# One column of every fourth chunk of a graph gather fetched by 128 single-row transfers on SP's queue

## The chip, the cores and the metric

The kernel runs on one core of a Trainium2 chip. The metric is the device time of one execution in microseconds (us), the median of three runs. Beside the runs stands one execution recorded by the hardware profiler; the rows below are from it.

## The reference

Two layers of a graph network on 12,500 nodes with 128 features and 200,000 edges, sorted by target node. Only the first matters here:

```
h = relu(layernorm(x))
msgs = h[src]                                   # 200,000 rows of 128 floats
neigh = segment_sum(msgs, dst, 12500)
x = x + relu(relu(((1 + eps) * h + neigh) @ W1 + b1) @ W2 + b2)
h = relu(layernorm(x))
x = x + attention(h, src, dst, edge_attr, ...)  # the second sweep
```

## The kernel before

There are two sweeps over the edges, one after the other; the diff touches the first (`gin_sweeps`). The edges lie in 98 chunks of 2,048 (`NCH`, `CHUNK`): 16 columns (`COLS`) of 128 edges, one edge to a partition. Of a chunk's messages GpSimd (POOL) fetches one column with one indirect DMA: 128 rows of 512 bytes, each at an address taken from a list of indices, into one of four buffers `hs0` to `hs3` (`gather_chunk`, L513). The table `h0` (in the trace `h_rows`) is written to DRAM in the first 105 us; the first four chunks are gathered from `x` itself and normed on chip.

Each engine runs its own instruction stream over the same steps (`over_stages`): eight steps written out, a hardware loop over four steps at a time, and the last steps written out. A step is named by the chunk f that POOL gathers in it. The others work on chunks further back, and two names look ahead: a2 is chunk f+2, a1 is f+1, p0 is f-1, r4 is f-4, a5 is f-5.

- POOL, in step f: waits for the index list of f and for the sums of chunk f-4, makes one tiny multiplication (`hold`, L507), and issues 16 gathers.
- SP, in step f: loads the index list of chunk a2 once the gathers of a2-4 have landed (L604), fetches the nodes' own rows for p0 (L628), and stores what chunks a5 and r4 produced: source rows (L634), key columns (L637), one row of key biases (L639), residual rows (L645). The address of most of these is a number that SP first loads from a table on chip into a register (`spot`, L431). SP does all this in program order.
- PE (TensorE), for a chunk: waits until its gathers have landed, clears the sums (L689), and makes 16 multiplications of a column of messages with a one-hot matrix (L695), then the layer's products for earlier chunks. VectorE (DVE) adds the sums to the accumulator (`add_sums`, L918); ScalarE (ACT) evicts and norms.

What SP does in a step, cut to its transfers:

```
if a2 and (a2.at is None or a2.at > 7): list_of(a2)
sp.dma_start(x[m.j][:, :, :], rows_at(a["x"], at))       # m = p0
sp.dma_start(rows_at(arow, at), A[m.j][:, :, :])         # m = a5
sp.dma_start(qk[:, bass.ds(at, MW)], kq[m.j][:, :])
sp.dma_start(ck[:, bass.ds(at, MW)], cq[m.j][:, :])
sp.dma_start(rows_at(res, at), r[m.j][:, :, :])          # m = r4
```

Of the kernel before, what the change touches and what calls it, by code (L numbers as in the profile page):

```python
# [67 lines left out]
MT = 2  # L68
MW = MT * P
STEPS = 7  # L70
assert (NCH - MID_PEEL) % 4 == 2 and 2 ** STEPS >= NCH and NCH * P == NP and NP >= MW
assert TILES % (2 * GT) == 0 and NBLK % PB == 0 and NCH % 4 == 2 and HALF <= 512

# [162 lines left out]
def head(nc, a, g, first, qk, ck, raw0, raw1, idx, weights):  # L236
# [4 lines left out]
    with ExitStack() as ctx:  # L241
# [29 lines left out]
        @block.sync  # L271
        def _(sp):
            sp.dma_start(g["idx0"][:, :], a["src_chunks"][0:1].rearrange("a p k -> p (a k)")).then_inc(idx_in, 16)
            sp.dma_start(by_block[:, :, :], a["dst_blocks"].rearrange("(k p) e -> p k e", p=PB)).then_inc(blocks_in, 16)
            sp.dma_start(idx[1][:, :], a["src_chunks"][1]).then_inc(idx1_in, 16)
            sp.dma_start(by_edge[:, :, :], a["dst_cols"].rearrange("p (b s) -> p b s", s=SUB)).then_inc(dst_in, 16)
            sp.dma_start(g["eps1"][:, :], a["eps"].to_broadcast([P, 1])).then_inc(eps_in, 16)
            for tile, rows in weights:
                sp.dma_start(tile[:, :], rows).then_inc(g["weights_in"], 16)
            for n in range(2, 5):  # L280
                sp.dma_start(idx[n % 4][:, :], a["src_chunks"][n]).then_inc(lists_in, 16)
            sp.wait_ge(zero_ready, 1)
            sp.dma_start(qk[:, NP:NW], zero[:, :]).then_inc(g["keys_out"], 16)
            sp.dma_start(ck[:, NP:NW], zero[0:1, :]).then_inc(g["keys_out"], 16)
            sp.wait_ge(start_ready, 2)
            sp.dma_start(first, start[:, :]).then_inc(g["start_out"], 16)
            sp.wait_ge(g["keys_out"], 32)
            sp.wait_ge(lists_in, 48)

        @block.gpsimd  # L290
        def _(gp):
# [222 lines left out]
                              in_offset=bass.IndirectOffsetOnAxis(ap=idx[:, k:k + 1], axis=0)).then_inc(done, 16)  # L514


def gin_sweeps(nc, a, g, h0, first, res, arow, qk, ck):


# [2 lines left out]
    with ExitStack() as ctx:  # L522
# [6 lines left out]
        weights += [(W[k], a[k]) for k in ("W1", "W2", "Wq", "WkT")]  # L529
        weights += [(W[k], a[k].rearrange("(a d) -> a d", a=1).to_broadcast([P, D])) for k in ("b2", "bt")]  # L530
        weights += [(col[k], a[k].rearrange("(d a) -> d a", a=1)) for k in ("b1", "bq", "bk", "gamma", "beta")]
        head(nc, a, g, first, qk, ck, raw0, raw1, idx, weights)
        span = nc.values_load(g["span"][0:1, 0:1], min_val=0, max_val=N + WIN)
        hs = [st.sb(f"hs{k}", [P, COLS, D]) for k in range(4)]
# [8 lines left out]
        kq, cq = st.two("kq", [P, MW]), st.two("cq", [1, MW])  # L543
        m1, m2 = moment_buffers(st, g, "m1"), moment_buffers(st, g, "m2")
        zeros = st.sb("zeros", [1, SPAN], BF16)
        sums = [st.ps(f"sums{j}") for j in range(2)]
        uy_bank, ta_bank, qk_bank, c_bank = (st.ps(k) for k in ("uy_bank", "ta_bank", "qk_bank", "c_bank"))
        u_ps, y_ps = uy_bank[:, 0:MW], uy_bank[:, MW:2 * MW]
# [4 lines left out]
        capped = hs[3][0:1, :, :].rearrange("p k d -> p (k d)")[:, 0:NBLK + NCH]  # L553
        w = {"capped": st.sem("w_capped"), "tables": st.sem("w_tables"), "spread": st.sem("w_spread")}
        held, lists_again = st.sem("held"), st.sem("lists_again")
        idx_in, gathered = ([st.sem(f"{k}_{n}") for n in range(4)] for k in ("idx_in", "gathered"))
        x_in, r_out, a_out, q_out = st.sem2("x_in"), st.sem2("r_out"), st.sem2("a_out"), st.sem2("q_out")
        hot_ready, sums_ready, added = st.sem("hot_ready"), st.sem("sums_ready"), st.sem("added")
# [10 lines left out]
        pe_regs = [nc.tensor.alloc_register(f"gin_win{b}") for b in range(BPC)]  # L569
        x_reg, r_reg, a_reg = (nc.sync.alloc_register(f"gin_{k}") for k in ("x_spot", "r_spot", "a_spot"))  # L570
        u_reg = nc.tensor.alloc_register("gin_u_spot")

        nc.vector.tensor_copy(g["spot"][:, :], g["spots"][0][:, :]).then_inc(spot_ready, 1)
        nc.vector.wait_ge(spot_ready, 1)
# [6 lines left out]
        x_groups = a["x"].rearrange("(g t p) d -> g p t d", t=GT, p=P)  # L581
        h_groups = h0.rearrange("(g t p) d -> g p t d", t=GT, p=P)
        one = lambda rows, G: rows[G:G + 1].rearrange("a p t d -> p (a t) d")
        landed = lambda m: 16 * (COLS * (m.g + (1 if m.k else 0)) - (AHEAD if m.k == 1 else 0))
        tail = [st.sem(f"tail{q}") for q in range(QUADS - 1)]
        listed = lambda m: 16 * (m.g - (0 if m.k else 1))
        raw_row = lambda n, k: raw0[:, k, :] if n == 0 else raw1[:, k, :] if n == 1 and k < AHEAD else hs[n % 4][:, k, :]
# [3 lines left out]
        with nc.Fori(0, span + 1, WIN):  # L591
            with nc.Block() as block:
                @block.sync
                def _(sp):
# [11 lines left out]
                    def first_lists():  # L606
                        for m in range(NCH - 4, NCH - 1):
                            sp.wait_ge(gathered[m % 4], landed(Chunk(None, m)))
                        for q in range(QUADS - 1):
                            sp.wait_ge(tail[q], 64)  # L610
                        for n in range(1, 5):
                            sp.dma_start(idx[n % 4][:, :], src[n]).then_inc(lists_again, 16)

                    def step(a2, a1, f, p0, p1, p2, r4, a5):
                        if a2 and a2.at is not None and 3 < a2.at < 7:
                            list_of(Chunk(None, a2.at + 1))
                        if a2 and (a2.at is None or a2.at > 7):
                            list_of(a2)
                        if f and f.at == 0:
                            for G in range(GROUPS):  # L620
                                node_rows(G)
                        if p0:
                            m = p0
                            if m.at == 0:
                                sp.wait_ge(w["tables"], 7)
                            at = spot(sp, x_reg, g, m.c)
                            wait(sp, s["x1"], m.c - 1)
                            sp.dma_start(x[m.j][:, :, :], rows_at(a["x"], at)).then_inc(x_in[m.j], 16)  # L628
                        if a5:
                            m = a5  # L630
                            at = spot(sp, a_reg, g, m.c)
                            wait_alone(sp, w["tables"], a_out[1 - m.j], 16 * (m.h + m.j))
                            wait(sp, s["a_sb"], m.c + 1)
                            sp.dma_start(rows_at(arow, at), A[m.j][:, :, :]).then_inc(a_out[m.j], 16)  # L634
                            wait_alone(sp, w["tables"], q_out[1 - m.j], 32 * (m.h + m.j))
                            wait(sp, s["k_sb"], m.c + 1)
                            sp.dma_start(qk[:, bass.ds(at, MW)], kq[m.j][:, :]).then_inc(keys_out if m.last else q_out[m.j], 16)  # L637
                            wait(sp, s["c_sb"], m.c + 1)
                            sp.dma_start(ck[:, bass.ds(at, MW)], cq[m.j][:, :]).then_inc(keys_out if m.last else q_out[m.j], 16)  # L639
                        if r4:  # L640
                            m = r4
                            at = spot(sp, r_reg, g, m.c)
                            wait_alone(sp, w["tables"], r_out[1 - m.j], 16 * (m.h + m.j))
                            wait(sp, s["r"], m.c + 1)
                            sp.dma_start(rows_at(res, at), r[m.j][:, :, :]).then_inc(r_out[m.j], 16)  # L645
                        if p2 and p2.at == NCH - 1:
                            first_lists()
                    over_stages(sp, step, 6, MID_PEEL, 2)
# [7 lines left out]
                def _(gp):  # L656
                    def step(f, bk, p1, p2, r4, a5):
                        if f and f.at != 0:
                            if f.at == 3:
                                gp.wait_ge(w["tables"], 7)  # L660
                            if f.at == RAW:
                                for u in range(4):
                                    gp.wait_ge(h_out[u], 16 * len(range(u, GROUPS, 4)))
                            wait(gp, idx_in[f.k], listed(f))
                            wait(gp, sums_ready, f.c - 3)
                            hold(gp, g, held, f.c - 1)
                            if f.last:
                                for q in range(QUADS - 1):
                                    gather_chunk(gp, idx[f.k], h0, hs[f.k], tail[q], cols=range(4 * q, 4 * q + 4))
                            else:  # L670
                                gather_chunk(gp, idx[f.k], a["x"] if f.at is not None and f.at < RAW else h0, hs[f.k], gathered[f.k],
                                             cols=range(AHEAD if f.at == 1 else 0, COLS))
                    over_stages(gp, step, 6, MID_PEEL)

                @block.tensor
                def _(pe):
# [3 lines left out]
                    def add_rows(bk):  # L680
# [9 lines left out]
                        for b in range(BPC):  # L690
# [1 line left out]
                            if bk.last and b % 2 == 0 and b // 2 < QUADS - 1:  # L692
                                pe.wait_ge(tail[b // 2], 64)
                            for k in range(b * SUB, (b + 1) * SUB):
                                mm = pe.matmul(sums[j][:, bass.ds(off, WIN)], hs[bk.k][:, k, :], hot[j][:, k, :],  # L695
                                               start=False, stop=True, skip_group_check=True)
                        mm.then_inc(sums_ready, 1)

# [65 lines left out]
                def _(act):  # L764
# [68 lines left out]
                            act.activation(hn[:, t, :], h2[:, t, :], ACT.Identity, bias=m2["shift"][:, t:t + 1],  # L833
                                           scale=m2["rstd"][:, t:t + 1]).then_inc(s["hn"], 1)

                    def step(f, bk, p1, p2, r4, a5):
                        if f and f.at == 0:
                            edge_rows(0)
                            for G in range(GROUPS):
# [23 lines left out]
                            norm2(p1)  # L863
                        if f and f.at is not None and 0 < f.at < RAW:
                            edge_rows(f.at)
                    over_stages(act, step, 6, MID_PEEL)

                @block.vector
                def _(v):
# [650 lines left out]
```

## Time and profile before

| what | us |
|---|---|
| median of 3 runs (lowest to highest) | 4064.28 (4064.09 to 4066.64) |
| the profiled execution | 4065.53 |
| its span, first to last instruction | 4063.9 |
| POOL busy, whole span | 3025.3 |
| PE busy, whole span | 3316.0 |

The span is 1.6 us shorter than the execution's time. A row of a timeline gives start and duration in us and the engine; SPq is SP issuing a transfer (the transfer itself goes on after that), POOL's gathers likewise. What stands in brackets is how long the engine was idle before, and what ended that; "issue" means that it waited for nothing that the profile shows. A row of a line's or tile's answer gives the smallest, median and largest duration in ns of its instructions; MOVE, FUSED_REGOPS and TENSOR_LOAD are the queue's own register instructions, the last a read of numbers from a table on chip into registers.

### The profile page before, as it was taken

To read this page: it belongs to the slowest core of one execution; us is meant where nothing else is said; L and a number is where in the kernel's file an instruction comes from. 1 tells how busy PE (TensorE), PEld (TensorE's weight loads), DVE (VectorE), ACT (ScalarE), POOL (GpSimd) and SP (SyncE) were. 2 spreads that over 40 slices of the span, in tenths; PEclk is the share of its full clock that TensorE was granted. 3 is DMA by queue.
4 is the path that set the end of the run, shared out by engine and by line. 5 is a ranking of instruction groups with operands and counts; after the bars stand their busy time and mean duration, and the time that the engine had idled before them with its cause. 6 is when DMAs were issued, how large, how long until landed. Compare 5 with 4: busy or idle time off the path is not lost.

```text
span 4063.9 us, 75137 instructions
## 1 busy us (share of the span) xinstructions
PE 3316.0 (82%) x19120; PEld 2587.6 (64%) x19121; DVE 1932.2 (48%) x6898; ACT 1590.9 (39%) x3223; POOL 3025.3 (74%) x3332
## 2 busy tenths in 40 slices
PE   1697777777767777777779999999999999999998
PEld 1465555555555555555557777777777777777776
DVE  5433222222222222222256666666666666666666
ACT  6433222222222222222244444444444444444444
POOL 6677777777777777777577777777777777777773
PEclk6555555555555555555589999999999999999998
DMA  6233333233333233333244444544454444444443
GB/s 189 70 83 82 80 79 79 78 79 78 79 78 78 79 79 78 79 78 79 72 124 140 139 140 137 142 136 142 134 141 140 140 139 138 139 139 139 139 139 91
DMA packets 390065, 446.29 MB, mean 110 GB/s; under 512 B 111768, under 2 KB 314734, under 8 KB 390000
## 3 DMA queue, kind: packets, MB, share of 16 engines
q0 software_dynamic: 100096, 205.20, 20.1%
q1 hardware_dynamic: 276940, 233.83, 19.4%
q10 hardware_dynamic: 12964, 6.53, 0.5%
q8 instruction: 25, 0.41, 0.0%
q14 instruction: 40, 0.33, 0.0%
HBM read 387.05 MB, written 58.21 MB: 110 GB/s over the span
## 4 chain that ended last, share of the span: by engine, by line
POOL 26%; issue 10%; PE 8%; DMA 4%; DVE 1%; SPq 1%; DVEq 0%; POOLq 0%; ACT 0%; ACTq 0%
POOL attention_t L513 26%; DMA attention_t<-source_rows,attention_idx 2%; PE attention_sc_q L1164 2%; PE attention_pre_ps L1141 2%; DMA attention_idx<-in_src_chunks 1%; PE attention_t_ps L1150 1%; PE attention_pre_ps L1137 1%; PE attention_sum_ps L1207 1%; PE attention_row_bank L1186 0%; PE attention_xm_bank L1227 0%; PE attention_xm_bank L1226 0%; DVE attention_masked L1431 0%; POOL spare L507 0%; SPq L1097 0%; DVE attention_rr L1454 0%
## 5 line engine op out<-in xcount | busy, mean ns | idle before, releaser
L513 POOL DMA_INDIRECT attention_t<-source_rows,attention_idx x1548 | 1478.4, 955 | 457.0 <-issue 448.1
L513 POOL DMA_INDIRECT gin_hs<-h_rows,gin_idx x1500 | 1428.6, 952 | 443.7 <-issue 443.4
L695 PE MATMUL gin_sums<-gin_hot,gin_hs 128*128 128x40 f32 x3136 | 684.8, 412 | 0.0
L695 PEld LDWEIGHTS gin_sums<-gin_hot,gin_hs 128*128 128x128 f32 x3136 | 670.4, 329 | 22.4 <-issue 21.9
L1278 ACT ACTIVATE attention_tT<-attention_pre_ps 128x512 f32<-128x512 f32 x391 | 233.5, 597 | 881.4 <-PE attention_pre_ps L1141 881.3
L1141 PE MATMUL attention_pre_ps<-attention_evT,attention_w_edge 128*128 128x512 f32 x782 | 419.7, 619 | 1.7 <-issue 1.7
L1164 PE MATMUL attention_sc_q<-attention_qw,attention_tT 128*128 x3128 | 410.9, 275 | 0.0
L1164 PEld LDWEIGHTS attention_sc_q<-attention_qw,attention_tT 128*128 128x128 f32 x3128 | 389.4, 196 | 0.0
L918 DVE TENSOR_TENSOR acc<-acc,gin_sums 128x264 f32 x98 | 42.1, 430 | 684.7 <-PE gin_sums L695 682.6
L1207 PE MATMUL attention_sum_ps<-attention_e_hot,attention_t 128*128 128x96 f32 x3072 | 365.9, 277 | 0.0
L1207 PEld LDWEIGHTS attention_sum_ps<-attention_e_hot,attention_t 128*128 128x128 f32 x3072 | 350.2, 192 | 11.9
L1137 PE MATMUL attention_pre_ps<-ident,attention_t 128*128 128x128 f32 x1564 | 255.9, 288 | 119.6 <-DMA attention_t<-source_rows,attention_idx 114.5
L798 ACT ACTIVATE gin_n_zT<-gin_c_bank,eps 128x256 f32<-128x256 f32 x98 | 46.5, 474 | 672.4 <-PE gin_c_bank L713 672.4
L1150 PEld LDWEIGHTS attention_t_ps<-ident,attention_tT 128*128 128x128 f32 x1564 | 195.2, 145 | 176.6 <-issue 167.1
L1416 DVE TENSOR_TENSOR attention_lines<-attention_lines,attention_row_bank 1x40 f32 x784 | 144.3, 184 | 337.3 <-issue 146.8
L689 PE MATMUL gin_sums<-gin_zeros 1*128 1x264 bf16 x98 | 36.4, 371 | 325.9 <-DMA gin_hs<-h_rows,gin_idx 293.7
L1137 PEld LDWEIGHTS attention_pre_ps<-ident,attention_t 128*128 128x128 f32 x1564 | 175.7, 145 | 161.3 <-issue 118.3
L689 PEld LDWEIGHTS gin_sums<-gin_zeros 1*128 1x128 bf16 x98 | 9.7, 99 | 399.0 <-issue 399.0
L1431 DVE TENSOR_TENSOR attention_masked<-attention_masked,attention_row_bank 128x80 f32<-128x80 f32 x784 | 126.6, 231 | 267.6 <-PE attention_row_bank L1186 267.3
L1150 PE MATMUL attention_t_ps<-ident,attention_tT 128*128 128x128 f32 x1564 | 245.9, 281 | 0.0
L1282 ACT ACTIVATE attention_t<-attention_t_ps 128x512 f32<-128x512 f32 x391 | 231.8, 593 | 27.2 <-PE attention_t_ps L1150 27.1
L491 ACT ACTIVATE gin_m_std<-gin_m_mv,ln_eps 128x2 f32<-128x2 f32 x294 | 85.1, 290 | 343.0 <-DVE gin_m_mv L485 342.5
(215 smaller groups left out, 5151.0 us busy)
## 6 DMA issues: line engine op xcount, KB each, us to landing
attention_evT<-in_edge_attr_cols SPq DMA_DIRECT2D x196, 512.0 KB
attention_t<-source_rows,attention_idx POOLq DMA_INDIRECT x1548
gin_hs<-h_rows,gin_idx POOLq DMA_INDIRECT x1500, 2.5
attention_qw<-qk_cols SPq DMA_DIRECT2D x98, 160.0 KB
attention_cw<-qk_bias_cols SPq DMA_DIRECT2D x98, 132.0 KB
attention_fade<-fades SPq DMA_DIRECT2D x98, 132.0 KB
gin_x<-in_x SPq DMA_DIRECT2D x98, 128.0 KB, 2.2
residual_rows<-gin_r SPq DMA_DIRECT2D x98, 128.0 KB, 2.1
```

Of the source, the lines that this page charges most:

```text
L491: act.activation(m["std"][:, :], m["mv"][:, :, 1], ACT.Sqrt, bias=g["ln_eps"][:, 0:1]).then_inc(s["std"], 1)
L513: gp.indirect_dma_start(out=out[:, k, :], out_offset=None, in_=rows[:, :], compute_op=op, in_offset=bass.IndirectOffsetOnAxis(ap=idx[:, k: ...
L695: mm = pe.matmul(sums[j][:, bass.ds(off, WIN)], hs[bk.k][:, k, :], hot[j][:, k, :], start=False, stop=True, skip_group_check=True)
L1137: pe.matmul(pre_ps[:, k * P:(k + 1) * P], t[f.k][:, 4 * q + k, :], g["ident"][:, :], is_transpose=True, start=(k == 0), stop=False, skip_g ...
L1141: pe.matmul(pre_ps[:, :], w_edge[:, :], evT[q // 2][:, 512 * (q % 2):512 * (q % 2 + 1)], start=False, stop=True, skip_group_check=True).th ...
L1150: mm = pe.transpose(t_ps[:, k * P:(k + 1) * P], tT[q % 2][:, k * P:(k + 1) * P], g["ident"][:, :])
L1164: mm = pe.matmul(sc_ps[:, o:o + WIDE], tT[q % 2][:, (n % 4) * P:(n % 4 + 1) * P], qw[j][:, bass.ds(off, WIDE)], start=True, stop=True)
L1207: mm = pe.matmul(sum_of(bk)[:, bass.ds(off, WIDE)], t[bk.k][:, k, :], e_hot[j][:, k, :], start=False, stop=True, skip_group_check=True)
L1278: act.activation(tT[q % 2][:, :], pre_ps[:, :], ACT.Gelu).then_inc(s["tT_sb"], 1)
L1282: act.activation(t[f.k][:, 4 * q:4 * q + 4, :].rearrange("p k d -> p (k d)"), t_ps[:, :], ACT.Copy).then_inc(s["t_sb"], 1)
L1416: v.tensor_tensor(some, some, row_bank[0:1, b * WIN:(b + 1) * WIN], ALU.max).then_inc(s["raised"], 1)
L1431: v.tensor_tensor(masked[j][:, cols, :], masked[j][:, cols, :], row_bank[:, bass.ds(off, WIN)].unsqueeze(1).to_broadcast([P, SUB, WIN]), A ...
```

## The change

For each fourth chunk from chunk 7 on (7, 11, ... 95: 23 chunks), column 15 is no longer gathered by POOL. SP loads that column's row numbers from a new list on chip (`lone_list`, 3,072 numbers, loaded once at the start), eight at a time into eight registers, and issues one transfer of one row (512 bytes, one partition) for each, 128 in all, into a new buffer `lone`. The 128 are split over four steps of SP: 32 at the end of the steps in which the chunk is a2, a1, f and p0. The first of the four waits for the sums of the chunk four before, which still reads `lone`. PE waits for the four quarters ahead of the chunk's last multiplication and reads `lone` in place of `hs`. `BY_ACT` is empty, so ACT issues none; its extra code does nothing. The cut diff:

```diff
+LONE = 3
+BY_SP, BY_ACT = (32, 32, 32, 32), ()
...
+            sp.dma_start(g["lone_list"][:, :], a["src_lone"]).then_inc(lists_in, 16)
...
+def alone(m):
+    return m is not None and m.k == LONE and (m.at is None or m.at > LONE)
+
+def rows_alone(eng, regs, g, m, table, out, spots, done):
+    for at in range(0, len(spots), len(regs)):
+        some = spots[at:at + len(regs)]
+        eng.load(regs[:len(some)], g["lone_list"][0:1, bass.ds(m.g * P + some[0], len(some))])
+        for reg, p in zip(regs, some):
+            row = eng.snap(reg, min_val=0, max_val=NP - 1)
+            eng.dma_start(out[p:p + 1, :], table[bass.ds(row, 1), :]).then_inc(done, 16)
...
+        g["lone_list"] = st.sb("lone_list", [1, NCH // 4 * P], I32)
+        lone = st.sb("lone", [P, D])
+        sp_rows, act_rows = ([e.alloc_register(f"gin_{k}_row{b}") for b in range(8)] for e, k in ((nc.sync, "sp"), (nc.scalar, "act")))
...
+                    def lone_rows(m, u):
+                        if u == 0:
+                            wait(sp, sums_ready, m.c - 3)
+                        if u == 0 and m.at == LONE + 4:
+                            for k in range(4):
+                                sp.wait_ge(h_out[k], 16 * len(range(k, GROUPS, 4)))
+                        at = sum(BY_SP[:u])
+                        rows_alone(sp, sp_rows, g, m, h0, lone, range(at, at + BY_SP[u]), lone_sp[u])
...
                             sp.dma_start(rows_at(res, at), r[m.j][:, :, :]).then_inc(r_out[m.j], 16)
+                        for u, m in enumerate((a2, a1, f, p0)):
+                            if alone(m):
+                                lone_rows(m, u)
...
-                                             cols=range(AHEAD if f.at == 1 else 0, COLS))
+                                             cols=range(AHEAD if f.at == 1 else 0, COLS - 1 if alone(f) else COLS))
...
-                                mm = pe.matmul(sums[j][:, bass.ds(off, WIN)], hs[bk.k][:, k, :], hot[j][:, k, :],
+                                by_row = alone(bk) and k == COLS - 1
+                                if by_row:
+                                    for u, n in enumerate(BY_SP):
+                                        wait(pe, lone_sp[u], 16 * n * bk.g)
...
+                                mm = pe.matmul(sums[j][:, bass.ds(off, WIN)], lone[:, :] if by_row else hs[bk.k][:, k, :], hot[j][:, k, :],
```

The line numbers below are each kernel's own; L513 of before is L517 in the change.

SP, one step of the loop. In the kernel before it is this, from the index list to the row of key biases, behind which the residual store (L645) ends the step:

```order
L604 DMA gin_idx<-in_src_chunks 128x16
L431 ISA
L431 TENSOR_LOAD pos
L628 ISA
L628 DMA gin_x<-in_x 128x2x128
L431 TENSOR_LOAD pos
L634 ISA
L634 DMA source_rows<-gin_A 128x2x128
L637 REGISTER_ALU
L637 DMA qk_cols<-gin_kq 128x256
L639 DMA qk_bias_cols<-gin_cq 1x256
```

In the change, from the residual store (L678, before L645) on, the same step goes on with one load of eight numbers and eight times an ISA (register arithmetic) and a one-row transfer, and that four times over, ahead of the next step's list:

```order
L678 DMA residual_rows<-gin_r 128x2x128
L530 ISA
L530 TENSOR_LOAD gin_lone_list
L532 ISA
L533 DMA gin_lone<-h_rows 1x128
L532 ISA
L533 DMA gin_lone<-h_rows 1x128
```

So each step of SP from 5 to 96 has 32 transfers, 32 register instructions and 4 loads more than before.

POOL, one turn of the loop in the change (four chunks). Before, each of the four rows of gathers reads x16:

```order
L517 DMA gin_hs<-h_rows,gin_idx 128x128 x16
L82 REGISTER_ALU
L511 TENSOR_TENSOR spare<-ones 1x1
L517 DMA gin_hs<-h_rows,gin_idx 128x128 x16
L82 REGISTER_ALU
L511 TENSOR_TENSOR spare<-ones 1x1
L517 DMA gin_hs<-h_rows,gin_idx 128x128 x15
L141 REGISTER_ALU
```

One gather of 64 is gone in each turn.

## Rows read from the trace of the kernel before

**Rows 1.** The page: slices of the span, PE, POOL and the granted clock.

```profile
PE   1697777777767777777779999999999999999998
...
POOL 6677777777777777777577777777777777777773
PEclk6555555555555555555589999999999999999998
```

**Rows 2.** Busy time of each engine in one stretch, in the first sweep.

```profile
core 0: us, PE busy (x) PEld busy (x) DVE busy (x) ACT busy (x) POOL busy (x), PEclk, DMA share, GB/s
400.00:1900.00 1500.00, 1089.41 (x4108) 836.92 (x4109) 424.68 (x1780) 416.05 (x1117) 1146.83 (x1267) 0.55 0.31 79
```

**Rows 3.** Timeline of POOL in the first sweep, from one chunk's end to the next.

```profile
1003.14 0.22 POOL L507 TENSOR_TENSOR spare<-ones 1x1 f32<-1x1 f32 x1
1003.52 0.98 POOL L513 DMA_INDIRECT gin_hs<-h_rows,gin_idx  x1 [0.15 <-issue]
1004.80 0.94 POOL L513 DMA_INDIRECT gin_hs<-h_rows,gin_idx  x1 [0.30 <-issue]
1006.05 0.95 POOL L513 DMA_INDIRECT gin_hs<-h_rows,gin_idx  x1 [0.30 <-issue]
...
1023.59 0.98 POOL L513 DMA_INDIRECT gin_hs<-h_rows,gin_idx  x1 [0.15 <-issue]
```

**Rows 4.** Who waited for whom, 340 to 1950 us: POOL, PE, SP's queue.

```profile
POOL gin_hs L513 <- issue: 377.8, 1280, 0.3
...
PE gin_sums L689 <- DMA gin_hs<-h_rows,gin_idx: 282.0, 72, 5.0
...
SPq L604 <- DMA gin_hs<-h_rows,gin_idx: 1191.6, 80, 16.1
```

**Rows 5.** Timeline of SP's queue, two steps of the first sweep.

```profile
1004.93 0.38 SPq L604 DMA_DIRECT2D gin_idx<-in_src_chunks  x1
1005.97 0.40 SPq L628 DMA_DIRECT2D gin_x<-in_x  x1
1006.99 0.40 SPq L634 DMA_DIRECT2D source_rows<-gin_A  x1
1007.63 0.37 SPq L637 DMA_DIRECT2D qk_cols<-gin_kq  x1
1008.09 0.29 SPq L639 DMA_DIRECT2D qk_bias_cols<-gin_cq  x1
1009.54 0.39 SPq L645 DMA_DIRECT2D residual_rows<-gin_r  x1
1024.96 0.37 SPq L604 DMA_DIRECT2D gin_idx<-in_src_chunks  x1
...
1029.37 0.38 SPq L645 DMA_DIRECT2D residual_rows<-gin_r  x1
```

**Rows 6.** Two one-row transfers on SP's queue, all instances: min/median/max ns.

```profile
L639 SPq DMA_DIRECT2D qk_bias_cols<-gin_cq x98: 283/292/324, 166.0 to 2035.9; - x98
...
L1037 SPq DMA_DIRECT2D attention_bv<-in_bv x1: 288/288/288, 2038.9 to 2038.9; - x1
```

**Rows 7.** Timeline of SP's queue in the second sweep, two transfers with register arithmetic between.

```profile
2528.69 0.33 SPq L1074 DMA_DIRECT2D attention_wgt<-in_wgt_cols  x1
2529.22 0.33 SPq L1080 DMA_DIRECT2D attention_qw<-qk_cols  x1
```

**Rows 8.** Loads of registers from a table: one number on SP, eight on PE.

```profile
L450 SPq TENSOR_LOAD <-places x98: 263/270/452, 2053.0 to 3987.3; - x98
...
L455 PEldq TENSOR_LOAD <-places x196: 587/592/1028, 48.3 to 4007.5; - x196
```

**Rows 9.** Timeline of DVE: adding the sums of chunks 3, 7, 8, 95 and 97.

```profile
174.93 0.43 DVE L918 TENSOR_TENSOR acc<-acc,gin_sums 128x264 f32 x1 [4.30 <-PE gin_sums L695]
...
237.62 0.43 DVE L918 TENSOR_TENSOR acc<-acc,gin_sums 128x264 f32 x1 [4.10 <-PE gin_sums L695]
254.25 0.43 DVE L918 TENSOR_TENSOR acc<-acc,gin_sums 128x264 f32 x1 [4.08 <-PE gin_sums L695]
...
1979.34 0.43 DVE L918 TENSOR_TENSOR acc<-acc,gin_sums 128x264 f32 x1 [7.36 <-PE gin_sums L695]
...
2016.63 0.43 DVE L918 TENSOR_TENSOR acc<-acc,gin_sums 128x264 f32 x1 [4.11 <-PE gin_sums L695]
```

**Rows 10.** The index lists (L604) on SP's queue: from issue to landing.

```profile
DMA to landing us min/median/max: 1.6/1.7/6.0
```

More of the change, by code:

```diff
@@ L70 @@
 STEPS = 7
+LONE = 3
+BY_SP, BY_ACT = (32, 32, 32, 32), ()
+assert sum(BY_SP) + sum(BY_ACT) == P
 assert (NCH - MID_PEEL) % 4 == 2 and 2 ** STEPS >= NCH and NCH * P == NP and NP >= MW
@@ L287, in _ @@
             sp.wait_ge(g["keys_out"], 32)
-            sp.wait_ge(lists_in, 48)
+            sp.wait_ge(lists_in, 64)
         @block.gpsimd
@@ L555, in gin_sweeps @@
         held, lists_again = st.sem("held"), st.sem("lists_again")
+        lone_sp, lone_act = ([st.sem(f"{k}_{u}") for u in range(len(n))] for k, n in (("lone_sp", BY_SP), ("lone_act", BY_ACT)))
         idx_in, gathered = ([st.sem(f"{k}_{n}") for n in range(4)] for k in ("idx_in", "gathered"))
@@ L583, in gin_sweeps @@
         one = lambda rows, G: rows[G:G + 1].rearrange("a p t d -> p (a t) d")
-        landed = lambda m: 16 * (COLS * (m.g + (1 if m.k else 0)) - (AHEAD if m.k == 1 else 0))
+        landed = lambda m: (16 * ((COLS - 1) * m.g + COLS) if m.k == LONE else
+                            16 * (COLS * (m.g + (1 if m.k else 0)) - (AHEAD if m.k == 1 else 0)))
         tail = [st.sem(f"tail{q}") for q in range(QUADS - 1)]
@@ L694, in add_rows @@
                             for k in range(b * SUB, (b + 1) * SUB):
-                                mm = pe.matmul(sums[j][:, bass.ds(off, WIN)], hs[bk.k][:, k, :], hot[j][:, k, :],
+                                by_row = alone(bk) and k == COLS - 1
+                                if by_row:
+                                    for u, n in enumerate(BY_SP):
+                                        wait(pe, lone_sp[u], 16 * n * bk.g)
+                                    for u, n in enumerate(BY_ACT):
+                                        wait(pe, lone_act[u], 16 * n * bk.g)
+                                mm = pe.matmul(sums[j][:, bass.ds(off, WIN)], lone[:, :] if by_row else hs[bk.k][:, k, :], hot[j][:, k, :],
                                                start=False, stop=True, skip_group_check=True)
@@ L834, in norm2, with lone_rows, step @@
                                            scale=m2["rstd"][:, t:t + 1]).then_inc(s["hn"], 1)
-                    def step(f, bk, p1, p2, r4, a5):
+                    def lone_rows(m, u):
+                        if u == 0:
+                            wait(act, sums_ready, m.c - 3)
+                        if u == 0 and m.at == LONE + 4:
+                            for k in range(4):
+                                act.wait_ge(h_out[k], 16 * len(range(k, GROUPS, 4)))
+                        at = sum(BY_SP) + sum(BY_ACT[:u])
+                        rows_alone(act, act_rows, g, m, h0, lone, range(at, at + BY_ACT[u]), lone_act[u])
+                    def step(a2, a1, f, bk, p1, p2, r4, a5):
                         if f and f.at == 0:
@@ L865, in step @@
                             edge_rows(f.at)
-                    over_stages(act, step, 6, MID_PEEL)
+                        for u, m in zip(range(len(BY_ACT)), (a2, a1, f)):
+                            if alone(m):
+                                lone_rows(m, u)
+                    over_stages(act, step, 6, MID_PEEL, 2)
                 @block.vector
@@ L1501 @@
         "src_chunks": np.ascontiguousarray(chunked(src, 0).reshape(NCH, P, COLS)),
+        "src_lone": np.ascontiguousarray(chunked(src, 0).reshape(NCH, P, COLS)[LONE::4, :, COLS - 1]).reshape(1, NCH // 4 * P),
         "dst_cols": cols(chunked(dst, N)),
```

## The prediction

> **What bounds the kernel now.** I read the slices first: PE is busy at seven tenths and more through the first half and nine in the second, POOL at seven throughout [rows 1]. The change touches the first half alone, so the averages of the page say nothing about it, and I took a stretch of the first sweep by itself: there POOL is busy 1147 of 1500 us and PE 1089, at a granted clock of 0.55 [rows 2], close to the lower of TensorE's two levels (1.2 of 2.4 GHz). Neither is full, so the waits must decide. POOL waits for nothing but "issue", 0.3 us before each gather [rows 3, 4]: its gathers follow each other every 1.25 us (1004.80, 1006.05), 16 of them with the tiny multiplication in about 20.05 us (1003.52 to 1023.59). PE waits for POOL's gathers, 282 us in 72 waits, and SP for the same, 1191.6 us in 80 [rows 4]. So a step of the first sweep is POOL's 20 us, PE has about 4 us of slack in it, and SP about 15.
>
> **What goes.** 23 gathers at 1.25 us [rows 3] are 28.7 us off POOL's stream. While POOL is the bound, this is the whole gain: 0.7%.
>
> **What SP gets.** Its stream is what I price, since SP does everything in order and each of its 92 steps from 5 to 96 gets 32 rows and 4 loads.
>
> - Its own work in a step runs from the list to the end of the residual store: 5.00 us in one step (1004.93 to 1009.93) and 4.79 in the next [rows 5], 4.9 on average, with 0.19 of register instructions ahead of the first transfer: **5.1 us**. It waits in it for the gathers alone.
> - A row: the transfer itself holds SP's queue 0.29 us, as both one-row transfers of the trace do, with a constant address and with one from a register [rows 6]. Between two transfers of which the second has a new address worked out in registers, the gap is 2529.22 - 2529.02 = 0.19 to 0.20 us [rows 7]. The change has exactly this between its rows (one ISA each), so 0.29 + 0.19 = **0.48 us a row**, 15.4 us for 32. The lowest row is the step from L637 to L639, which use one address: 0.09 us between, 0.38 a row [rows 5]. That is not this pattern, and I keep it for a rival.
> - A load of eight numbers: none on SP in the trace. On PE eight take 0.59 us, on SP one takes 0.27 [rows 8], so eight cost about 0.32 more. From L628 to L634 the gap is 0.62 with a one-number load in it, without the 0.19 of register work 0.43: the lower end, as if eight cost what one does. Behind the one-row store L639 the gap is 1.16 [rows 5]; less 0.19 and plus 0.32 that is 1.29, the upper end. The middle, 0.43 + 0.32 = 0.75, has no delay behind a one-row transfer; three of four loads stand behind one, but the 1.16 also holds more waits than the 0.62. I take **0.95 us**, 3.8 for four.
>
> The step of SP is then 5.1 + 15.4 + 3.8 = **24.3 us**, and POOL's would be about 19.7 (20.05 less a quarter of 1.25). SP becomes the bound, and the 28.7 us on POOL are worth nothing: POOL will wait for sums or lists.
>
> **Who waits.** PE needs the last quarter of a chunk's rows ahead of its last multiplication; SP issues it at the end of the step before. With SP late, PE stands in front of that multiplication in each fourth chunk, and the other three run at PE's own pace, which has room: 16.63 us from chunk 7 to 8, when POOL was ahead [rows 9]. SP's new wait, for the sums of the chunk before that used `lone`, should cost little: they come 1.7 us of landing [rows 10] plus under 1 us after the last row, and SP meanwhile does 5.1 us of its own step. If that cover failed, at most 5 us in each of 23 chunks would be added. PE's four extra waits and the list's load at the start (one transfer more, ahead of a wait of SP for other engines' tables) I cost at nothing: PE waits there anyway, and the start's price, uncovered, is one transfer, some 0.4 us [rows 5].
>
> **The sum.** The first rows can go when chunk 3 is summed, 174.93 us, in step 5 [rows 9]: its batch takes 19.2 us, to 194.6. Then 91 steps of 24.3 us: 2211.3, so the last row is issued at 2405.9. With 1.7 us to land and 0.9 for multiplication and adding, the sums of chunk 95 are added at 2408.5, where they were at 1979.3. The last two chunks are gathered by then and go at PE's 16.63 us each, 2441.8 for chunk 97, where it was 2016.63 [rows 9]. So the second sweep starts 425 us later. It isn't touched. Against the profiled execution's 4065.5 us, which is 1.3 above the median of the runs, that is **4490 us**, 10% slower.
>
> **Bounds.** With loads at 0.43 the step is 22.2 us, 92 times 2.1 less: 4297. With 1.29 it is 25.7: 4615. A row off by 0.01 us is 0.32 a step and 29 us in all. That gives 4270 to 4645.
>
> **Rival 1: hidden, faster.** If SP's batch stays under 19.7 - 5.1 = 14.6 us (0.46 us a row, its share of a load included), POOL stays the bound and the time is 4065.5 - 28.7 = 4037. For it: SP idles 15 us in a step now [rows 4], and with the lowest rows, 0.38 a row and 0.43 / 8 = 0.05 for its load, a batch is 13.8 us. Against it: each row has its own address, and the four loads at their lower end with rows of 0.48 already make 17.1 us. The Trainium skill, "DMA: Bandwidth & Descriptors", section "Issuing engines are not separate DMA queues", has the rule behind this rival: the sequencer's time to start a transfer is "usually small relative to the DMA itself"; by it the time is 4037. The trace speaks against leaning on it: a list needs 1.7 us to land, but SP has issued the next transfer by then [rows 5, 10], so of many small transfers in a row the issue is what adds up. Chance 0.06.
>
> **Rival 2: each row holds up the next, much slower.** The gap behind the one-row store is 1.16 us where the gap with the same kind of load behind a larger transfer is 0.62 [rows 5]. If some 0.4 us of that were a stall after every one-row transfer, which decides as soon as it hits rows and not loads alone, a row is 0.88, a step 37.1 us, and 92 times 12.8 more makes 5668. Against it: a transfer only sends, and what was seen to be late is a load, which must read. The Trainium skill, same page, section "Why a DMA increments its semaphore by 16 and not by 1", says that of a transfer spread over fewer than 16 engines the issuing sequencer writes the rest of the increment itself; no row here shows how many engines a one-row transfer uses. Chance 0.08.
>
> **Rival 3: even.** Costs that meet near 14.6 us a batch: within 0.2% of 4065, about 8 us, which is what a measurement of this kernel can tell from no change. The window is narrow, 14.6 us give or take 0.1. Chance 0.02. That the change does not do what it says is no rival: the order shows 15 gathers and 128 one-row transfers in each turn of the loop.
>
> **Chances.** The forecast has 0.84, rival 1 0.06, rival 2 0.08, rival 3 0.02. Faster 0.06, same 0.02, slower 0.92. The range is the forecast's own, 4270 to 4645; it leaves out the rivals, 0.16, and a little of the forecast's edges.
>
> **What would show it.** In the profile after: steps of SP's queue in the first sweep 24 us apart from list to list, with no idle time before the list (the 1191.6 us of waits on gathers gone); one-row transfers 0.48 us apart within eight, about 1.4 from one eight to the next; PE waiting for transfers into `lone` in each fourth chunk; POOL waiting for sums or lists where it waited for nothing; 23 gathers fewer; the second sweep as long as before. Rows under 0.4 us apart and SP still waiting for gathers would mean rival 1; rows 0.9 apart rival 2. Loads much off 0.95 move the time by 92 x 4 = 368 times the difference.

## The result, and the profile after

| | before | after |
|---|---|---|
| median, us (runs) | 4064.42 (4) | 4354.85 (4) |
| lowest to highest, us | 4064.09 to 4066.64 | 4351.46 to 4356.85 |
| ratio, 95% interval | | 1.0718 [1.0706, 1.0731] |
| profiled execution and its span, us | 4065.53, 4063.9 | 4354.31, 4352.7 |

The change makes the kernel 290 us slower. The forecast was 4490 us in a range of 4270 to 4645: the direction and the mechanism came as foretold, the size was 135 us too large.

The page after, slices of the span and the engines' sums:

```profile
PE 3237.3 (74%) x19120; PEld 2506.3 (58%) x19121; DVE 1931.4 (44%) x6898; ACT 1590.9 (37%) x3223; POOL 3020.6 (69%) x3309
...
PE   1765556654755556566557999999999999999998
...
POOL 6666666666666666666634777777777777777774
...
PEclk5555655556565555655566999999999999999998
```

PE stood at seven tenths and more in the first sweep and POOL at seven [rows 1]; now PE mostly shows five and six and POOL six. No engine that counts as "busy" has become fuller. Only the queue that issues has, and that one has no line on the page. A second change is easy to miss: a slice is 109 us now and was 102, and yet the first sweep ends in the 22nd slice, where it ended in the 20th; from there on the slices look as before.

The waits show it. Who waited for whom after, 340 to 2200 us (engine, line, releaser: us in total, times, longest):

```profile
PE gin_sums L737 <- DMA gin_lone<-h_rows: 433.9, 21, 24.6
DVE gin_A L957 <- DMA source_rows<-gin_A: 429.9, 60, 10.1
...
POOL gin_hs L517 <- issue: 405.7, 1283, 0.5
...
POOL spare L511 <- DMA gin_idx<-in_src_chunks: 187.2, 76, 3.2
...
POOL spare L511 <- PE gin_sums L737: 13.4, 5, 2.9
```

PE's 282 us of waits for gathers [rows 4] are gone from the list, and so are SP's 1191.6: the same question for SP's queue has no row at all. In their place PE stands in front of the last multiplication of each fourth chunk, 434 / 21 = 20.7 us each time, and POOL, which waited for nothing, waits 187 us for index lists that SP issues late. DVE's 430 us belong to SP as well: its stores of source rows are late, so their buffers come free late. That last one I had not foreseen. The time follows SP's step alone in the runs below, so I take it to cost nothing of its own; no run tests it by itself.

SP's queue itself, timeline after, two steps of the loop (start, duration, x32 is 32 transfers from the first one's start to the last one's end):

```profile
1013.20 0.37 SPq L628 DMA_DIRECT2D gin_idx<-in_src_chunks  x1
1014.42 0.40 SPq L661 DMA_DIRECT2D gin_x<-in_x  x1
...
1017.79 0.38 SPq L678 DMA_DIRECT2D residual_rows<-gin_r  x1
1019.23 16.30 SPq L533 DMA_DIRECT2D gin_lone<-h_rows  x32
1035.84 0.37 SPq L628 DMA_DIRECT2D gin_idx<-in_src_chunks  x1
...
1041.77 16.31 SPq L533 DMA_DIRECT2D gin_lone<-h_rows  x32
1059.04 0.38 SPq L628 DMA_DIRECT2D gin_idx<-in_src_chunks  x1
```

SP works through without a pause. Its own part, list to the end of the residual store, is 1018.17 - 1013.20 = 4.97 us (5.00 and 4.79 before, [rows 5]). From there to the end of the last row, the batch, it is 1035.53 - 1018.17 = **17.36 us**, and 0.31 more to the next list. In the second step that gap is 0.96 (1058.08 to 1059.04). Over the steps between 340 and 1880 us the three parts are 5.05, 17.35 and 0.45 us on average, 22.85 together. The gap is 0.97 in every fourth step and 0.2 to 0.3 in the others; the loop has four steps to a turn, but whether its turn is the cause no run shows.

How long one row takes is seen in narrower pieces of the same timeline (the first eight rows, the eighth alone, and the ninth, behind the next load), and in all instances of the three lines (smallest, median and largest duration in ns):

```profile
1019.23 3.29 SPq L533 DMA_DIRECT2D gin_lone<-h_rows  x8
1022.29 0.23 SPq L533 DMA_DIRECT2D gin_lone<-h_rows  x1
1023.54 0.27 SPq L533 DMA_DIRECT2D gin_lone<-h_rows  x1
```

```profile
L533 SPq DMA_DIRECT2D gin_lone<-h_rows x2944: 224/228/324, 174.8 to 2270.2; - x197
...
L530 SPq TENSOR_LOAD <-gin_lone_list x368: 533/694/852, 174.1 to 2263.7; - x184
...
L532 SPq FUSED_REGOPS  x2944: 44/44/56, 174.7 to 2270.1; - x197
```

A row holds the queue 0.228 us (the first of a load's eight up to 0.32). From the first row of the eight to the eighth it is 22.29 - 19.23 = 3.06; less 0.08 for the longer first one that is 0.426 us a row. From the eighth to the ninth it is 1.25, with a load of 0.69 in it: a load costs 1.25 - 0.43 + 0.08 = 0.90 us more than a row alone. All in all the 92 batches run from 174.8 to 2270.2: less 16.1 for the last batch's own rows, (2095.4 - 16.1) / 91 = **22.85 us a step**, where the gathers had set 19.92 (the lists from 198.0 to 1930.9 us, 87 steps; MOVE is the register instruction ahead of each list with a computed address). The lists before:

```profile
L604 SPq MOVE gin_idx<-in_src_chunks x88: 29/29/29, 198.0 to 1930.9; - x88
```

The sums of chunks 95 and 97, DVE after (in brackets the idle time before and what ended it):

```profile
2272.31 0.43 DVE L972 TENSOR_TENSOR acc<-acc,gin_sums 128x264 f32 x1 [15.86 <-PE gin_sums L737]
...
2305.44 0.43 DVE L972 TENSOR_TENSOR acc<-acc,gin_sums 128x264 f32 x1 [4.13 <-PE gin_sums L737]
```

Before, 97 was added at 2016.63 [rows 9]. From there to the end of the span it was 2047.3 us (4063.9 - 2016.63), and it is 2047.3 now (4352.7 - 2305.44). The whole 289 us lie in the first sweep; that they are SP's is what the experiments test.

### The profile page after: what moved, and what is told of

Its sections match the earlier page's. It is cut to its first block and busy times, and to the rows that moved or that the text cites. A ratio compares the mean times of both kernels' runs of the same rounds, so it can differ in the third digit from the quotient of the medians.

```text
span 4352.7 us, 84781 instructions
## 1 busy us (share of the span) xinstructions
PE 3237.3 (74%) x19120; PEld 2506.3 (58%) x19121; DVE 1931.4 (44%) x6898; ACT 1590.9 (37%) x3223; POOL 3020.6 (69%) x3309
## 3 DMA queue, kind: packets, MB, share of 16 engines
q14 instruction: 152, 1.25, 0.1%
## 5 line engine op out<-in xcount | busy, mean ns | idle before, releaser
L517 POOL DMA_INDIRECT attention_t<-source_rows,attention_idx x1548 | 1477.1, 954 | 456.9 <-issue 449.9
L517 POOL DMA_INDIRECT gin_hs<-h_rows,gin_idx x1477 | 1425.7, 965 | 465.9 <-issue 465.6
L737 PE MATMUL gin_sums<-gin_hot,gin_hs 128*128 128x40 f32 x3090 | 594.3, 379 | 0.0
L737 PEld LDWEIGHTS gin_sums<-gin_hot,gin_hs 128*128 128x128 f32 x3090 | 580.6, 293 | 19.1 <-issue 14.9
L737 PE MATMUL gin_sums<-gin_hot,gin_lone 128*128 128x40 f32 x46 | 14.3, 411 | 475.7 <-DMA gin_lone<-h_rows 475.7
L737 PEld LDWEIGHTS gin_sums<-gin_hot,gin_lone 128*128 128x128 f32 x46 | 11.5, 312 | 478.2 <-issue 478.2
L511 POOL TENSOR_TENSOR spare<-ones 1x1 f32<-1x1 f32 x195 | 36.9, 189 | 331.4 <-DMA gin_idx<-in_src_chunks 202.8
L957 DVE TENSOR_TENSOR gin_A<-gin_ta_bank,gin_w_bt 128x256 f32<-128x256 f32 x98 | 40.7, 415 | 495.2 <-DMA source_rows<-gin_A 491.6
```

Source lines behind the costliest of these rows:

```text
L517: gp.indirect_dma_start(out=out[:, k, :], out_offset=None, in_=rows[:, :], compute_op=op, in_offset=bass.IndirectOffsetOnAxis(ap=idx[:, k: ...
L737: mm = pe.matmul(sums[j][:, bass.ds(off, WIN)], lone[:, :] if by_row else hs[bk.k][:, k, :], hot[j][:, k, :], start=False, stop=True, skip ...
```

## The experiments

All are edits of the changed kernel. The theory: SP's stream of instructions sets the step. The main rival: something else that the change brought (PE's wait in front of the last multiplication, the chunk's own latency, the missing gathers' place) does. Ratios are to the kernel before in runs on the same chip: 4064.42 us beside the change, 4071.61 beside e1_pool16, e_rows112, e_rows96 and e_mix, 4078.24 beside the other four; they lie up to 0.001 from the quotients of the medians shown here. "Batch" is read from one step of each profile as above, from the end of the residual store to the end of the last row; "step" is the time from the first list with a computed address to the last, divided by 87. The profiled executions of e_rows96 (4059.57) and e_mix4 (4030.08) were the highest and the lowest of their runs, so their steps carry that spread.

| kernel | SP's rows a step, loads | batch, us | step, us | median, us | ratio [95%] |
|---|---|---|---|---|---|
| the change | 32, 4 | 17.36 | 22.9 | 4354.85 | 1.0718 [1.0706, 1.0731] |
| e1_pool16 | 32, 4 | 17.37 | 22.8 | 4354.77 | 1.0701 [1.0684, 1.0717] |
| e_load16 | 32, 2 | 16.61 | 22.2 | 4304.98 | 1.0555 [1.0535, 1.0574] |
| e_mix | 23, 3 | 15.73 (12.82 in each fourth, 15.0 on average) | 20.5 | 4139.78 | 1.0171 [1.0157, 1.0185] |
| e_rows112 | 28, 4 | 15.09 | 20.7 | 4154.2 | 1.0207 [1.0192, 1.0223] |
| e_scaled8 | 32, 4 | 14.94 | 20.3 | 4125.36 | 1.0125 [1.0107, 1.0142] |
| e_scaled16 | 32, 2 | 13.92 | 19.6 | 4052.97 | 0.9946 [0.9931, 0.9962] |
| e_rows96 | 24, 3 | 12.98 | 19.6 | 4044.09 | 0.9924 [0.991, 0.9937] |
| e_mix4 | 24 and 20, 3 | 12.93 | 19.3 | 4043.23 | 0.992 [0.9906, 0.9935] |

**e1_pool16: POOL gathers all 16 columns again, SP still fetches the rows.** PE still waits for `lone`, but multiplies the gathered column.

```diff
...
-  cols=range(AHEAD if f.at == 1 else 0, COLS - 1 if alone(f) else COLS)
+  cols=range(AHEAD if f.at == 1 else 0, COLS)
...
-  mm = pe.matmul(..., lone[:, :] if by_row else hs[bk.k][:, k, :], ...)
+  mm = pe.matmul(..., hs[bk.k][:, k, :], ...)
```

> SP issues and PE awaits the 128 one-row transfers as in the change, but POOL gathers all 16 columns again and PE multiplies the gathered column. Theory (SP's issue work sets the step, 22.9 us, POOL's 20.05 us fits below it): the 23 gathers that were saved are worth nothing, so 4355 us, give or take 10. Rival A (POOL's stream still sets part of the time beside SP): the 28.7 us come back on top, 4383. Rival B (contention of row transfers with gathers is the cost): more than 4383.

The 23 gathers taken from POOL are worth nothing while SP sets the step: the medians are 4354.77 and 4354.85 us and the two intervals overlap, though POOL has all its old work; 28.7 us more would have been 0.007 more in the ratio. POOL had time to spare: between 340 and 1900 us it waits 159 us for index lists in the change and still 113 us here.

```profile
POOL spare L511 <- DMA gin_idx<-in_src_chunks: 113.0, 60, 2.8
```

That is the prediction's "the 28.7 us on POOL are worth nothing", shown.

**e_rows112 and e_rows96: fewer rows.** SP fetches 112 and 96 of the 128 rows; the last 16 and 32 are left out of the sums (zeros in their place).

```diff
-BY_SP, BY_ACT = (32, 32, 32, 32), ()
+BY_SP, BY_ACT = (28, 28, 28, 28), ()      # e_rows96: (24, 24, 24, 24)
...
+        nc.vector.memset(lone[:, :], 0.0).then_inc(spot_ready, 1)
```

> 28 rows a step in place of 32; the last 16 rows of the column are left out (zeros are added for them). Theory: SP's step shrinks by 4 x 0.42 and a little of the last load, to about 21.0 us, still over POOL's 19.75; 92 x 1.85 less, about 4185 us. Rival (PE's wait for the landing of late one-row transfers is the cost, whatever their number): above 4300.

> 24 rows and 3 loads a step; the last 32 rows of the column are left out (zeros are added for them). Theory: SP's step shrinks by 8 x 0.42 and one load group of 0.86 to about 18.6 us, under POOL's 19.75, so POOL is the bound again and the saved gathers count: 4064 - 29 = 4036 us. Rival (waiting for the landing): still slower than 4064.

From 32 rows to 28 the step falls by 2.2 us and the time by some 200, 92 times that; I had expected 1.85 and 170, so four rows are worth more than the price of a row and of the shorter load accounts for, and why is open. From 28 to 24 the batch loses 2.1 us more, the step only 1.1: it has reached POOL's. With 24 rows SP waits again. SP's queue in e_rows96, 340 to 1900 us:

```profile
SPq L628 <- DMA gin_hs<-h_rows,gin_idx: 59.6, 44, 2.8
SPq L529 <- PE gin_sums L737: 45.9, 15, 3.1
```

And then the change's gain is there: 0.9924 with an interval of 0.991 to 0.9937, where 28.7 us of 4065 would be 0.9929. All other parts of the change (the buffer, PE's waits, SP's new wait) are still in this kernel, so none of them costs more than about 0.1% of the time, the room that the interval leaves.

**e_mix: all 128 rows, 36 of them issued by ACT.**

```diff
-BY_SP, BY_ACT = (32, 32, 32, 32), ()
+BY_SP, BY_ACT = (23, 23, 23, 23), (12, 12, 12)
```

> All 128 rows, 23 a step on SP in four steps and 12 a step on ACT in three. Theory: SP's step is about 18.2 us, hidden; ACT gets some 6.5 us at the end of its step, in which it idles about 7.5 us before the next sums: hidden or nearly, 4036 to 4050. Rival (ACT's lateness reaches PE's chain): each of 69 ACT batches costs up to 6.5 us beyond PE's 3.5 us of slack, some 4100 to 4250.

A miss, and 4139.78 us lies in the range that I had given to the rival, ACT. But SP has fewer rows than in e_rows96 and yet a longer batch. What got longer is its loads. All loads in e_mix, and beside them those of e_rows112:

```profile
L530 SPq TENSOR_LOAD <-gin_lone_list x276: 541/1799/2003, 173.8 to 2048.8; - x138
...
L530 ACTq TENSOR_LOAD <-gin_lone_list x138: 500/617/747, 186.3 to 2028.3; - x138
```

```profile
L529 SPq TENSOR_LOAD <-gin_lone_list x368: 461/692/875, 169.6 to 2063.6; - x184
```

A load on SP takes 1.80 us at the median here and 0.69 there. With batches of 23 the loads of the first step begin at places 0, 8 and 16 of the chunk's list, those of the other three at 23, 46 and 69 and onward by eight: none of these is a multiple of four. Within the one kernel, loads of 8, 8 and 7 numbers each time, first in a step of the second kind and then in the one of the first kind:

```profile
L530 SPq TENSOR_LOAD <-gin_lone_list x3: 1633/1839/1899, 1013.3 to 1024.3; - x3
...
L530 SPq TENSOR_LOAD <-gin_lone_list x3: 698/824/1099, 1077.3 to 1085.9; - x3
```

So the place from which a load reads seems to decide, at equal sizes. A multiple of eight is not needed: in e_rows112 batches begin at 28 and 84 too, and its loads take 0.69 at the median and 0.875 at most. The next run tests it; why it is so, no run shows.

**e_mix4: the same with every load at a multiple of four.**

```diff
+BY_SP, BY_ACT = (24, 24, 24, 20), (12, 12, 12)
```

> As the mixed run, but with 24, 24, 24 and 20 rows a step on SP and 12 on ACT in three, so that each load of eight numbers begins at a multiple of four numbers in the list. In the mixed run SP's loads took 1.8 us where they began at odd multiples and 0.7 elsewhere. Theory (the place of the numbers is what made them slow): loads at 0.7 us, SP's step about 18.6 us, under POOL's 19.75: 23 gathers less, about 0.992 of before. Rival (ACT's issuing beside SP made SP's loads slow, or ACT's batch delays PE): still 1.01 to 1.02 of before.

ACT issues the same 36 rows as in e_mix, so it was not ACT that cost the time there. SP's loads are back at 0.70 us, SP waits again, and this is the best version with all 128 rows:

```profile
L530 SPq TENSOR_LOAD <-gin_lone_list x276: 462/696/827, 173.6 to 1931.2; - x138
```

```profile
SPq L628 <- DMA gin_hs<-h_rows,gin_idx: 70.6, 45, 2.4
SPq L530 <- PE gin_sums L737: 50.1, 20, 3.1
```

It beats the kernel before by 0.8% and the change by 7%: the idea of the change is good for what POOL saves, as long as SP's part of the rows fits into POOL's step.

**e_load16: sixteen numbers a load.** Two loads a step in place of four.

```diff
-  sp_rows, act_rows = ([e.alloc_register(f"gin_{k}_row{b}") for b in range(8)] ...
+  sp_rows, act_rows = ([e.alloc_register(f"gin_{k}_row{b}") for b in range(16)] ...
```

> All 128 rows on SP, loaded by two loads of 16 numbers a step in place of four of eight. Theory (the step is the sum of SP's instructions): a load of 16 takes 0.69 + 8 x 0.04 = 1.0 us, so the step falls by 4 x 0.86 - 2 x 1.17 = 1.1 us to 21.8, 92 x 1.1 = 101 us less: about 1.047 of before. Rival (SP's loads are hidden behind its transfers, which set the pace): 1.07 as the change.

Faster than the change, by less than I expected: the step falls by 0.6 us and not by 1.1, mostly since a load of sixteen takes 1.19 us, not 1.0, twice a step. The rest is the gap ahead of the next list, 0.56 us here on average and 0.45 in the change; its cause is open. All loads of e_load16:

```profile
L530 SPq TENSOR_LOAD <-gin_lone_list x184: 987/1194/1312, 171.8 to 2201.8; - x184
```

**e_scaled8 and e_scaled16: less register work a row.** The list is multiplied once, on DVE at the start, by a row's 512 bytes, and the table is read as bytes. Then the register holds the place itself, and in the trace one register instruction of some 0.15 us serves eight rows, in place of one of 0.044 us for each; the same in e_scaled16, which also has e_load16's edit and so two behind each load.

```diff
...
+    flat = table.rearrange("(a n) d -> a (n d)", a=1).bitcast(U8)
...
+        places = [eng.snap(reg, min_val=0, max_val=(NP - 1) * ROW) for reg in regs[:len(some)]]
+        for place, p in zip(places, some):
+            eng.dma_start(out[p:p + 1, :].bitcast(U8), flat[:, bass.ds(place, ROW)]).then_inc(done, 16)
...
+        nc.vector.tensor_scalar(g["lone_list"][:, :], g["lone_list"][:, :], float(ROW), None, ALU.mult).then_inc(spot_ready, 1)
```

> All 128 rows on SP; the list is multiplied by the row's 512 bytes once, by DVE at the start, and the address is used as loaded, so one register instruction for eight rows takes the place of one for each row. Theory: a row falls from 0.42 to about 0.33 us, the step by some 2.5 us to 20.3 to 20.8, still over POOL's 19.75: 1.013 to 1.026 of before. Rival (the transfer itself sets the pace, the register work is hidden): 1.07 as the change.

> The scaled list and loads of 16 together. Theory: both savings add, step 19.2 to 19.7 us, just under POOL's: all 128 rows on SP are hidden and the 23 gathers count, 0.992 to 1.003 of before. Rival: the savings don't add, over 1.01.

Both came as expected, e_scaled8 at the lower edge. SP's queue in e_scaled16, sixteen rows behind one load, and the waits of POOL and PE, 340 to 1900 us:

```profile
1000.72 5.28 SPq L536 DMA_DIRECT2D gin_lone<-h_rows  x16
```

```profile
POOL gin_hs L519 <- issue: 362.2, 1226, 0.3
POOL gin_hs L519 <- DMA gin_idx<-in_src_chunks: 1.8, 6, 0.3
...
PE gin_sums L741 <- DMA gin_lone<-h_rows: 248.8, 20, 14.7
```

Less 0.23 for the last transfer and 0.08 for the longer first one, 4.97 us for 15 rows are 0.33 us a row; so the register instruction of 44 ns and the gap that it brings cost 0.43 - 0.33 = 0.10 us of every row (the transfer itself still holds the queue 0.228 us at the median). The 0.15 us ahead of each eight rows take a fifth of that back. With the fewer loads that is enough for all 128 rows on SP alone: POOL again waits for next to nothing. PE still waits for `lone` there, 248.8 us in 20 waits, but no longer at the cost of POOL's step. At 0.9946 the gain is a little less than the whole 28.7 us (0.9929): SP shows no wait either, the two are even.

## Why the prediction was right, and where its size was off

- **What bounds (right).** "SP becomes the bound, and the 28.7 us on POOL are worth nothing." SP has no wait left, PE stands before `lone`, POOL waits for lists; e1_pool16 gives POOL its gathers back for nothing, and e_rows112 takes the time down by 92 times what it takes off SP's step.
- **Start and end of the sum (right).** The first rows were forecast for 174.93 us and start at 174.8. From the sums of chunk 95 to those of 97 it was to be 33.3 us and is 33.13. The second sweep is as long as before. That SP's wait for the sums and PE's four waits cost nothing held too: e_rows96 and e_mix4 have them and still gain.
- **SP's own work (0.4 too small).** 5.1 us forecast, of which 0.19 ahead of the list. Measured are 5.05 on average and 0.45 ahead of the list, 5.5, because of the long gap in every fourth step.
- **A load (right, by luck in the middle).** 0.95 forecast, 0.90 measured. Loads behind a one-row transfer aren't as late as the upper end of 1.29 supposed: the load itself takes 0.69, near PE's 0.59 [rows 8].
- **A row (the step that failed).** "The transfer itself holds SP's queue 0.29 us, as both one-row transfers of the trace do." In a stream of its own kind it holds it 0.228. The gap behind it was priced exactly: 0.426 - 0.228 = 0.20, forecast 0.19 from the second sweep's two transfers [rows 7]. So a row is 0.43 and not 0.48, 32 of them 13.6 and not 15.4 us. The batch, rows and loads, is 17.35 for 19.2, the own work gives 0.4 back, and the step is 22.85 for 24.3: 91 times 1.45 is 132 of the 135 us that the forecast was too long. That the range held the time is partly luck. It gave a row 0.01 us either way, 29 us in all, and the row was off by five times that; the width came from the loads, which then lay near the middle, and the own work took part of the error back.
- **Rival 1, hidden.** Refuted for the change as it stands, but its break-even, a batch of 14.6 us, was close: in the table the batches of 14.94 and more are slower than before, and those of 13.92 and less faster. At 13.92 SP and POOL are already even, so it lies nearer 14, since the own work takes 5.5 us of a step and not 5.1. The Trainium skill, "DMA: Bandwidth & Descriptors", section "Issuing engines are not separate DMA queues", calls the sequencer's time "usually small relative to the DMA itself". For one row the trace agrees: 0.23 us of issue, while the sweep's last row, issued at 2270.2, was waited for until PE's multiplication at 2271.55, 1.35 us later. For the kernel's time, leaning on it would have given rival 1's 4037 us, and 4354.85 was measured, because 32 such times and what goes with them stand in one queue in each step.
- **Rival 2, each row holds up the next.** Refuted: rows 0.43 apart, not 0.88.
- **Rival 3, even.** Refuted: the change is 290 us from even.

## What to carry to other kernels

Price a split into many small transfers on the queue that issues them, register work and loads included, against the time that this queue is idle in one step; here 0.43 us a row and 0.9 a load made a batch of 17.4 us where about 14 were free, and the page of the profile has no line for it. Where it doesn't fit, two ways worked here: give a part to a second queue with idle time (e_mix4), or put the scaled address in the table, so that no address arithmetic stands between two transfers, and load more numbers at once (e_scaled16). Of the second way neither half was enough by itself. Take the price of a transfer from one that stands among its own kind if there is one: the two single ones that I used held the queue a quarter longer.

## What was not expected of the hardware

- A transfer of one row of 512 bytes holds SP's queue 0.228 us behind another of its kind, and up to 0.32 as the first behind a load (the change). The two single ones before held it 0.288 and 0.292 [rows 6], and the first of them is a row of 512 bytes too, behind larger transfers. So size alone does not make the difference; whether it is the transfer that stands ahead was not tried.
- A load of registers from a table on chip: 0.46 us for four numbers (the least of e_rows112 and e_mix4), 0.69 for eight (the change), 1.19 for sixteen (e_load16); and 1.6 to 1.9 us for seven or eight when the first does not lie at a multiple of four numbers (e_mix).
- The gap between a batch's last row and the next list is 0.2 to 0.3 us in three steps of four and 0.97 in the fourth (the change), without a wait in the profile. It adds to the step; its cause is open.
